# Scores and maxima in pairs, value and denominator batches in halves

## The chip, the core and the metric

The kernel runs on one core of one Trainium2 chip. The metric is the device time of one execution in microseconds, from launch to end. Five engines work side by side on that core: TensorE (matrix products), VectorE, ScalarE, GpSimd and SyncE, which issues most of the DMAs. Each runs its own list of instructions in order, and they wait for each other through semaphores.

## The reference, cut to what matters

A one-layer language model over 2 sequences of 2048 tokens, width 1024:

```python
h = b + sum(Wt[k][ctx[..., k]] for k in range(4))            # four table rows a token
h = h + attn(layernorm(h))                                   # 32 heads of 32, 8 key/value heads
h = h + ffn(layernorm(h))                                    # one product with a merged weight

# attention, for each of 2 x 32 heads; four heads share one key/value head
scores = q @ k.T / sqrt(32)                                  # 2048 x 2048, after rotary embedding
scores = where(causal, scores, -1e20)
out = softmax(scores, axis=-1) @ v
```

All of it is float32. The matrix products of attention's scores use a split of each operand in a high and a low part, stacked along the contracted rows: 96 rows are 3 x 32.

## The kernel before, in words

Three parts run one after the other: `part_a` (tables, layer norm, projections, rotary), `part_b` (attention) and `part_c` (output projection and last layer). The change is in `part_b` alone.

`part_b` works through 16 groups (`GROUPS`), a group being four query heads (`GROUP`) and the key/value head they share. The first and the last group are written out, the 14 between them are one loop (`groups`, L517). Queries are cut in four chunks of 512 (`QC`, `CT`), keys in tiles of 128. A **step** (`STEPS`, `score_steps`) is one chunk c of queries against one key tile kt, for the four heads: 40 steps a group. Each chunk begins with its four diagonal steps, in which only 512, 384, 256 and 128 queries see the key tile; then come its 4c full steps of 512. In a diagonal step a second small matmul with a mask is added to each score (L798).

The softmax subtracts the row maximum ahead of the exponential, so the maxima are computed first, one group's worth some 20 steps ahead (`LEAD`). For them queries are the rows: `MAXES` lists units (chunk, key chunk, query tile, head), 160 a group. TensorE computes one unit into one of four banks of PSUM (`row_scores`, L756), VectorE reduces it over its up to 512 keys into one column of `mpart` (`row_max`, L708). Behind the last unit of a chunk VectorE reduces `mpart` to `mcol`; TensorE transposes that (`turn`, L772), `TURN_AFTER` = 5 units later; VectorE splits the row in high and low part, and SyncE sends both into rows 96 and 97 of the queries `qs`, so that the score matmul of 98 rows subtracts the maximum by itself. `max_entries` writes units and turns in one list, spread over the steps; `entries_in` says which belong to a step.

In a step TensorE issues (`group`, L847):

- for each head h a score matmul into bank h mod 2 (`scores`, L785), which waits until ScalarE has taken the score two before it; behind it a quarter of the step's maxima entries (as a rule one), each of which waits until VectorE has done the entry four before it;
- after head 1 the value product of the step before the last (`values`, L801, `VALUE_LAG` = 2). Its output is 32 columns of the array wide for each head, and the four heads stand side by side in the array: four matmuls in float32, issued together, which the trace shows as eight records. I call this a value batch;
- at the end of every second step the denominators of a pair of steps (`denominators`, L814, `DEN_LAG` = 4): the same form, with ones in place of values, on the sum of two steps' probabilities that GpSimd made (L656). In a diagonal pair a batch over the 128 columns that only one step has stands ahead of it (L823).

```python
if not (is_first(g) and u < SCORE_BANKS):
    pe.wait_ge(exp_done, unit + u - (SCORE_BANKS - 1))
...
for h in range(GROUP):
    scores(g, unit, s, h)
    for more, n in entries[len(entries) * h // GROUP:len(entries) * (h + 1) // GROUP]:
        give(g + more, ring + more * NE, n)
    if h == GROUP // 2 - 1:
        lagging_values(g, unit, s)
lagging_denominators(g, pair, s)
```

ScalarE takes the exponentials one by one (`exps`, L667). At a chunk's end it also copies the value sums out of PSUM (`take_o`, L675) and the denominators (`take_den`, L680); the latter stands behind the first exponential of the step `DEN_LAG` + 1 behind the chunk's last (L691). The opening batch of the next chunk waits for these copies.

Of the kernel before, what the change touches and what calls it, by code (L numbers as in the profile page):

```python
# [17 lines left out]
P = 128  # L18
# [19 lines left out]
CT = 512  # L38
# [378 lines left out]
def max_units():  # L417

    return [(c, kc, t, h) for c in range(QC) for kc in range(c + 1) for t in range(TPC) for h in range(GROUP)]


STEPS, MAXES = score_steps(), max_units()
# [6 lines left out]
SCORE_BANKS, MAX_BANKS = 2, 4  # L429
VALUE_LAG, DEN_LAG = 2, 4  # L430
LEAD, FIRST_LEAD = 20, 14
TURN_AFTER = 5
# [30 lines left out]
def part_b(nc, q_hi, q_lo, k_hi, k_lo, v_dram, o_dram, den_dram, ident_in, mask_qk, mask_kq):  # L463

    with ExitStack() as ctx:
# [12 lines left out]
        mpart = sb("mpart", [P, GROUP * TPC, QC], F32)  # L478
        mcol = sb("mcol", [P, GROUP * TPC], F32)
# [7 lines left out]
        mx_ps = ctx.enter_context(nc.psum_tensor("mx_ps", [P, MAX_BANKS, CT], F32))  # L487
# [214 lines left out]
        def _(dve):  # L702
# [5 lines left out]
            def row_max(g, ring, n, unit):  # L708
# [3 lines left out]
                if unit - 1 in LAST_MAX or (unit == 0 and not is_first(g)):  # L712
                    dve.wait_ge(max_all, g * QC + c)
                nc.vector.tensor_reduce(mpart[:, h * TPC + t, kc:kc + 1], mx_ps[:, n % MAX_BANKS, 0:w], AX, ALU.max  # L714
                                        ).then_inc(max_done, 1)
                if unit in LAST_MAX:
                    dve.wait_ge(max_done, ring + n + 1)
                    nc.vector.tensor_reduce(mcol[:], mpart[:, :, 0:c + 1], AX, ALU.max).then_inc(max_all, 1)

            def maxima_rows(g, ring, n, c):  # L720

                mt_ps = mx_ps[0:GROUP * TPC, n % MAX_BANKS, 0:P]
# [8 lines left out]
            def take(g, ring, n):  # L731
                _, what, which = ENTRIES[n]
                if what == "max":
                    row_max(g, ring, n, which)
                else:
                    maxima_rows(g, ring, n, which)
# [13 lines left out]
        def _(pe):  # L750
            ring_count, unit_count = pe.alloc_register("pe_ring_count"), pe.alloc_register("pe_unit_count")
            step_count, pair_count = pe.alloc_register("pe_step_count"), pe.alloc_register("pe_pair_count")
# [3 lines left out]
            def row_scores(g, ring, n, unit):  # L756

                c, kc, t, h = MAXES[unit]
# [6 lines left out]
                out = mx_ps[:, n % MAX_BANKS, 0:w]  # L765
                mm = nc.tensor.matmul(out, qs[c][0:K_ROWS, h, t * P:(t + 1) * P],  # L766
                                      k_max[0:K_ROWS, kc * CT:kc * CT + w], start=True, stop=not diagonal)
                if diagonal:
                    mm = nc.tensor.matmul(out[:, w - P:w], identr, mqk, start=False, stop=True)  # L769
                mm.then_inc(max_ready, 1)  # L770

            def turn(g, n, c):  # L772
                pe.wait_ge(max_all, g * QC + c + 1)
                nc.tensor.transpose(mx_ps[0:GROUP * TPC, n % MAX_BANKS, 0:P], mcol[:], ident[:]).then_inc(max_ready, 1)

            def give(g, ring, n):
                _, what, which = ENTRIES[n]
                if not (is_first(g) and n < MAX_BANKS):
                    pe.wait_ge(max_done, ring + n - (MAX_BANKS - 1))
                if what == "max":  # L780
                    row_scores(g, ring, n, which)
# [504 lines left out]
```

## Time and profile before

| | us |
|---|---|
| median of 3 runs | 4025.11 |
| lowest, highest | 4018.99, 4042.11 |
| the profiled execution | 4027.74 |
| its span, first to last instruction | 4025.9 |

| engine | busy us | share of the span |
|---|---|---|
| TensorE, matmuls | 3776.8 | 94% |
| TensorE, weight loads | 2433.5 | 60% |
| VectorE | 2292.9 | 57% |
| ScalarE | 1626.7 | 40% |
| GpSimd | 1589.7 | 39% |

The profile is of one execution. Its page gives busy time by engine, then the span in 40 slices; other views group instructions by line and shape, sum them over a stretch, or list them in order of time. Matmul records overlap, since the array takes the next one while the last drains: a busy share near 100% isn't the array at its peak, and the pace is read from starts. Attention runs from about 740 us to 3200 us of the span.

### The profile page before, as it was taken

How to read it: one execution, taken by the hardware profiler on the slowest of the kernel's cores; microseconds unless marked ns; L12 is line 12 of the kernel's file. 1: busy time of each engine (PE TensorE's matmuls, PEld its weight loads, DVE VectorE, ACT ScalarE, POOL GpSimd, SP SyncE). 2: the span in 40 equal slices, each digit the busy share in tenths (PEclk: the TensorE clock that was granted, in tenths of full speed). 3: DMA queues.
4: the chain of work that ended last, by engine and by line, in shares of the span. 5: the costliest groups of instructions: out<-in, count | busy, mean ns of one | idle time of the engine just before them, and what ended most of it. 6: DMA issues, size and time to landing. Idle time of an engine off the chain costs nothing. (4 is left out here: it accounts for less than half of the span.)

```text
span 4025.9 us, 69672 instructions
## 1 busy us (share of the span) xinstructions
PE 3776.8 (94%) x22272; PEld 2433.5 (60%) x22272; DVE 2292.9 (57%) x3912; ACT 1626.7 (40%) x3068; POOL 1589.7 (39%) x525
## 2 busy tenths in 40 slices
PE   2889888899999999999999999999999779999999
PEld 2777777655555555555555555555555248888887
DVE  3666656676566566566566566566566144443443
ACT  2222222155555555555555555555555521010110
POOL 5222330045544544544544544545544513232322
PEclk9999999799999999999999999999999979999999
DMA  8877785411111111111111111111110243334432
GB/s 242 209 182 193 202 200 133 97 44 47 33 46 47 33 46 47 33 46 47 33 46 47 33 46 47 33 46 47 33 46 25 70 138 94 93 87 94 90 96 65
DMA packets 240124, 325.95 MB, mean 81 GB/s; under 512 B 62795, under 2 KB 139595, under 8 KB 239859
## 3 DMA queue, kind: packets, MB, share of 16 engines
q1 hardware_dynamic: 221426, 255.22, 23.7%
q0 software_dynamic: 18432, 67.12, 7.6%
q8 instruction: 177, 2.90, 0.3%
q14 instruction: 89, 0.72, 0.1%
HBM read 223.67 MB, written 97.52 MB: 80 GB/s over the span
## 5 line engine op out<-in xcount | busy, mean ns | idle before, releaser
L714 DVE TENSOR_REDUCE mpart<-mx_ps 128x1 f32<-128x512 f32 (+3 forms) x2560 | 1455.1, 606 | 841.4 <-PE mx_ps L769 455.3
L672 ACT ACTIVATE probs<-st_ps 128x512 f32<-128x512 f32 (+3 forms) x2560 | 1297.7, 533 | 1093.6 <-PE st_ps L798 535.7
L656 POOL TENSOR_TENSOR sums<-probs 128x2048 f32<-128x2048 f32 (+1 forms) x320 | 1182.6, 3696 | 1256.8 <-PE den_ps L827 1171.3
L795 PE MATMUL st_ps<-qs,k_score 98*128 98x512 f32 (+3 forms) x2560 | 1087.2, 428 | 31.2 <-issue 25.3
L766 PE MATMUL mx_ps<-k_max,qs 96*128 96x512 f32 (+3 forms) x2560 | 985.4, 393 | 14.5 <-POOL consts_r L647 14.1
L795 PEld LDWEIGHTS st_ps<-qs,k_score 98*128 98x128 f32 x2560 | 482.1, 189 | 814.5 <-ACT probs L672 659.6
L810 PE MATMUL o_ps<-probs,vs 128*32 128x512 f32 (+3 forms) x5120 | 606.9, 546 | 0.0
L766 PEld LDWEIGHTS mx_ps<-k_max,qs 96*128 96x128 f32 x2560 | 495.1, 195 | 48.2 <-POOL consts_r L647 14.3
L202 POOL DMA_INDIRECT hbuf<-in_tok_table,idx x128 | 194.1, 1517 | 352.3 <-ACT xn L233 231.2
L1030 POOL TENSOR_TENSOR h<-h,bb 128x1024 f32<-128x1024 f32 x32 | 105.1, 3283 | 543.2 <-DVE xn_c L1128 543.2
L386 PE MATMUL qk_ps<-x_hi,w_hi 128*128 128x512 f32 x640 | 259.7, 406 | 51.2 <-ACT rotation L245 31.8
L827 PE MATMUL den_ps<-sums,ones 128*32 128x512 f32 (+2 forms) x2560 | 284.1, 516 | 2.2 <-POOL sums L656 2.2
L386 PE MATMUL qk_ps<-x_lo,w_hi 128*128 128x512 f32 x640 | 256.6, 401 | 0.0
L386 PE MATMUL qk_ps<-x_hi,w_lo 128*128 128x512 f32 x640 | 255.9, 400 | 0.0
L798 PE MATMUL st_ps<-consts_r 128*128 128x128 f32 x1024 | 246.1, 240 | 5.9 <-issue 5.9
L769 PE MATMUL mx_ps<-consts_r 128*128 128x128 f32 x1024 | 246.0, 241 | 0.0
L769 PEld LDWEIGHTS mx_ps<-consts_r 128*128 128x128 f32 x1024 | 201.8, 197 | 28.4
L798 PEld LDWEIGHTS st_ps<-consts_r 128*128 128x128 f32 x1024 | 198.5, 194 | 22.6 <-issue 8.2
L1116 DVE TENSOR_TENSOR h<-oc_ps,h_in 128x1024 f32<-128x1024 f32 x32 | 39.2, 1225 | 289.6 <-PE oc_ps L1177 289.6
L810 PEld LDWEIGHTS o_ps<-probs,vs 128*32 128x32 f32 x5120 | 101.5, 108 | 151.7 <-ACT probs L672 84.2
L1054 ACT ACTIVATE std_c<-var_c 128x1 f32<-128x1 f32 x32 | 6.5, 203 | 434.2 <-DVE var_c L1123 434.2
L386 PEld LDWEIGHTS qk_ps<-x_hi,w_hi 128*128 128x128 f32 x640 | 125.1, 195 | 82.1 <-ACT rotation L245 34.7
(103 smaller groups left out, 3819.9 us busy)
## 6 DMA issues: line engine op xcount, KB each, us to landing
qs<-q_hi_scratch SPq DMA_DIRECT2D x128, 256.0 KB, 4.5
h_scratch<-hbuf SPq DMA_DIRECT2D x32, 512.0 KB, 3.5
q_hi_scratch<-rot_hi SPq DMA_DIRECT2D x64, 256.0 KB, 2.6
q_lo_scratch<-rot_lo SPq DMA_DIRECT2D x64, 256.0 KB, 3.3
qs<-q_lo_scratch SPq DMA_DIRECT2D x64, 256.0 KB, 5.5
o_scratch<-o_sb SPq DMA_DIRECT2D x64, 256.0 KB
o_in<-o_scratch SPq DMA_DIRECT2D x32, 512.0 KB, 4.4
o_in<-recip_scratch SPq DMA_DIRECT2D x128, 128.0 KB, 7.9
```

Of the source, the lines that this page charges most:

```text
L202: nc.gpsimd.indirect_dma_start(hbuf[:, t, :], None, tables[k], bass.IndirectOffsetOnAxis(ap=idx[:, j:j + 1], axis=0), compute_op=ALU.bypas ...
L386: mm = nc.tensor.matmul(qk_ps[:, f % 2, :], w[a], x[b], start=(c == 0 and k == 0), stop=(c == DC - 1 and k == 2))
L656: nc.gpsimd.tensor_tensor(sums[:, p % SUM_SLOTS, :, j * P:CT], a, b, ALU.add).then_inc(sum_done, 1)
L672: nc.scalar.activation(probs[:, s % SLOTS, h, j * P:CT], st_ps[:, u % SCORE_BANKS, 0:CT - j * P], ACT.Exp, scale=float(HD) ** -0.5).then_i ...
L714: nc.vector.tensor_reduce(mpart[:, h * TPC + t, kc:kc + 1], mx_ps[:, n % MAX_BANKS, 0:w], AX, ALU.max).then_inc(max_done, 1)
L766: mm = nc.tensor.matmul(out, qs[c][0:K_ROWS, h, t * P:(t + 1) * P], k_max[0:K_ROWS, kc * CT:kc * CT + w], start=True, stop=not diagonal)
L769: mm = nc.tensor.matmul(out[:, w - P:w], identr, mqk, start=False, stop=True)
L795: mm = nc.tensor.matmul(st_ps[:, u % SCORE_BANKS, 0:w], k_score[0:M_ROW + 2, kt * P:(kt + 1) * P], qs[c][0:M_ROW + 2, h, j * P:CT], start= ...
L798: mm = nc.tensor.matmul(st_ps[:, u % SCORE_BANKS, 0:P], identr, mkq, start=False, stop=True)
L810: mm = nc.tensor.matmul(o_ps[h * HD:(h + 1) * HD, j * P:CT], vs[:, kt, :], probs[:, s % SLOTS, h, j * P:CT], start=s in FIRST_OF, stop=s i ...
L827: mm = nc.tensor.matmul(den_ps[h * HD:(h + 1) * HD, at:CT], ones[:], sums[:, p % SUM_SLOTS, h, at:CT], start=False, stop=closing)
L1030: nc.gpsimd.tensor_tensor(h1[:, s, :], h1[:, s, :], bb[:], ALU.add).then_inc(h1b_done, 1)
```

## The change

Maxima are listed by pairs of heads (`max_pairs`, 80 a group). A pair has a slot of two banks, of which there are two; TensorE issues its two matmuls behind one wait, and VectorE reduces both with one instruction that writes two columns of `mpart`. A turn comes 3 pairs behind its chunk. Scores are issued in pairs too: heads 0 and 1, then 2 and 3, into the two banks, each pair behind one wait for all exponentials issued so far. Each half of a step is a score pair, half of the step's maxima entries, and a part of the value batch, now of the step before (`VALUE_LAG` = 1): columns up to 384 (`VALUE_SPLIT`) in the first half, the rest in the second; the wait for its exponentials is gone, since the score pair ahead has waited for them. Behind the second half comes half of a denominator batch, every step. The diff, without the renamings on VectorE and with its other declarations cut:

```diff
+def max_pairs():
...
+    return [(c, kc, t, h) for c in range(QC) for kc in range(c + 1) for t in range(TPC) for h in range(0, GROUP, 2)]
...
-SCORE_BANKS, MAX_BANKS = 2, 4
-VALUE_LAG, DEN_LAG = 2, 4
+SCORE_BANKS, MAX_SLOTS = 2, 2
+VALUE_LAG, DEN_LAG = 1, 4
+VALUE_SPLIT = 3 * P
 LEAD, FIRST_LEAD = 20, 14
-TURN_AFTER = 5
+TURN_AFTER = 3
...
-        mpart = sb("mpart", [P, GROUP * TPC, QC], F32)
+        mpart = sb("mpart", [P, GROUP, TPC, QC], F32)
...
-        mx_ps = ctx.enter_context(nc.psum_tensor("mx_ps", [P, MAX_BANKS, CT], F32))
+        mx_ps = ctx.enter_context(nc.psum_tensor("mx_ps", [P, MAX_SLOTS, 2, CT], F32))
...
-                nc.vector.tensor_reduce(mpart[:, h * TPC + t, kc:kc + 1], mx_ps[:, n % MAX_BANKS, 0:w], AX, ALU.max
+                nc.vector.tensor_reduce(mpart[:, h:h + 2, t, kc], mx_ps[:, n % MAX_SLOTS, :, 0:w], AX, ALU.max
                                         ).then_inc(max_done, 1)
-                if unit in LAST_MAX:
...
-            def row_scores(g, ring, n, unit):
-
-                c, kc, t, h = MAXES[unit]
-                if t == 0 and h == 0 and kc == 0:
+            def pair_scores(g, n, pair):
+
+                c, kc, t, first_head = MAXES[pair]
+                if t == 0 and first_head == 0 and kc == 0:
                     pe.wait_ge(q_loaded[c], LOAD * (g + 1))
-                if t == 0 and h == 0 and kc == c:
+                if t == 0 and first_head == 0 and kc == c:
                     pe.wait_ge(k_max_loaded[c], LOAD * (g + 1))
                 diagonal = kc == c
                 w = (t + 1) * P if diagonal else CT
-                out = mx_ps[:, n % MAX_BANKS, 0:w]
-                mm = nc.tensor.matmul(out, qs[c][0:K_ROWS, h, t * P:(t + 1) * P],
-                                      k_max[0:K_ROWS, kc * CT:kc * CT + w], start=True, stop=not diagonal)
-                if diagonal:
-                    mm = nc.tensor.matmul(out[:, w - P:w], identr, mqk, start=False, stop=True)
+                for k in range(2):
+                    out = mx_ps[:, n % MAX_SLOTS, k, 0:w]
+                    mm = nc.tensor.matmul(out, qs[c][0:K_ROWS, first_head + k, t * P:(t + 1) * P],
+                                          k_max[0:K_ROWS, kc * CT:kc * CT + w], start=True, stop=not diagonal)
+                    if diagonal:
+                        mm = nc.tensor.matmul(out[:, w - P:w], identr, mqk, start=False, stop=True)
                 mm.then_inc(max_ready, 1)
 
...
-                if not (is_first(g) and n < MAX_BANKS):
-                    pe.wait_ge(max_done, ring + n - (MAX_BANKS - 1))
+                if not (is_first(g) and n < MAX_SLOTS):
+                    pe.wait_ge(max_done, ring + n - (MAX_SLOTS - 1))
...
-            def scores(g, unit, s, h):
+            def scores(g, unit, s, first_head):
 
                 c, kt, j = STEPS[s]
-                u, w = s * GROUP + h, CT - j * P
+                w = CT - j * P
                 diagonal = kt >= c * TPC
-                if s in FIRST_OF and h == 0:
+                if s in FIRST_OF and first_head == 0:
                     pe.wait_ge(m_rows, 32 * (g * QC + c + 1))
                     pe.wait_ge(k_score_loaded[c], LOAD * (g + 1))
-                if not (is_first(g) and u < SCORE_BANKS):
-                    pe.wait_ge(exp_done, unit + u - (SCORE_BANKS - 1))
-                mm = nc.tensor.matmul(st_ps[:, u % SCORE_BANKS, 0:w], k_score[0:M_ROW + 2, kt * P:(kt + 1) * P],
-                                      qs[c][0:M_ROW + 2, h, j * P:CT], start=True, stop=not diagonal)
-                if diagonal:
-                    mm = nc.tensor.matmul(st_ps[:, u % SCORE_BANKS, 0:P], identr, mkq, start=False, stop=True)
-                mm.then_inc(st_ready, 1)
-
-            def values(g, unit, s):
+                if not (is_first(g) and s == 0 and first_head == 0):
+                    pe.wait_ge(exp_done, unit + s * GROUP + first_head)
+                for h in range(first_head, first_head + 2):
+                    bank = h % SCORE_BANKS
+                    mm = nc.tensor.matmul(st_ps[:, bank, 0:w], k_score[0:M_ROW + 2, kt * P:(kt + 1) * P],
+                                          qs[c][0:M_ROW + 2, h, j * P:CT], start=True, stop=not diagonal)
+                    if diagonal:
+                        mm = nc.tensor.matmul(st_ps[:, bank, 0:P], identr, mkq, start=False, stop=True)
+                    mm.then_inc(st_ready, 1)
+
+            def values(g, s, part):
 
                 c, kt, j = STEPS[s]
-                pe.wait_ge(exp_done, unit + GROUP * (s + 1))
-                if s in FIRST_OF:
+                if s in FIRST_OF and part == 0:
                     pe.wait_ge(v_loaded[c], 16 * (g + 1))
                     if not (is_first(g) and c == 0):
                         pe.wait_ge(o_copied, g * QC + c)
-                for h in range(GROUP):
-                    mm = nc.tensor.matmul(o_ps[h * HD:(h + 1) * HD, j * P:CT], vs[:, kt, :],
-                                          probs[:, s % SLOTS, h, j * P:CT], start=s in FIRST_OF, stop=s in LAST_OF)
-                mm.then_inc(pv_done, 1)
-
-            def denominators(g, pair, p):
+                lo, hi = ((j * P, VALUE_SPLIT), (max(j * P, VALUE_SPLIT), CT))[part]
+                if lo < hi:
+                    for h in range(GROUP):
+                        mm = nc.tensor.matmul(o_ps[h * HD:(h + 1) * HD, lo:hi], vs[:, kt, :],
+                                              probs[:, s % SLOTS, h, lo:hi], start=s in FIRST_OF and part == 0,
+                                              stop=s in LAST_OF and part == 1)
+                if part == 1:
+                    mm.then_inc(pv_done, 1)
+
+            def denominators(g, pair, p, part):
 
                 c, kt, j = STEPS[2 * p]
                 diagonal, opening, closing = kt >= c * TPC, 2 * p in FIRST_OF, 2 * p + 1 in LAST_OF
-                pe.wait_ge(sum_done, pair + p + 1)
-                if opening and not (is_first(g) and c == 0):
-                    pe.wait_ge(den_copied, g * QC + c)
-                if diagonal:
+                alone = (j * P, (j + 1) * P) if diagonal else (0, 0)
+                half = (j * P + CT) // 2 if diagonal else CT // 2
+                if part == 0:
+                    pe.wait_ge(sum_done, pair + p + 1)
+                    if opening and not (is_first(g) and c == 0):
+                        pe.wait_ge(den_copied, g * QC + c)
+                    if diagonal:
+                        for h in range(GROUP):
+                            nc.tensor.matmul(den_ps[h * HD:(h + 1) * HD, alone[0]:alone[1]], ones[:],
+                                             probs[:, 2 * p % SLOTS, h, alone[0]:alone[1]], start=opening, stop=False)
+                lo, hi = ((alone[1], half), (half, CT))[part]
+                if lo < hi:
                     for h in range(GROUP):
-                        nc.tensor.matmul(den_ps[h * HD:(h + 1) * HD, j * P:(j + 1) * P], ones[:],
-                                         probs[:, 2 * p % SLOTS, h, j * P:(j + 1) * P], start=opening, stop=False)
-                at = (j + 1) * P if diagonal else 0
-                for h in range(GROUP):
-                    mm = nc.tensor.matmul(den_ps[h * HD:(h + 1) * HD, at:CT], ones[:],
-                                          sums[:, p % SUM_SLOTS, h, at:CT], start=False, stop=closing)
-                mm.then_inc(den_done, 1)
-
...
-                    for h in range(GROUP):
-                        scores(g, unit, s, h)
-                        for more, n in entries[len(entries) * h // GROUP:len(entries) * (h + 1) // GROUP]:
+                    for part in range(2):
+                        scores(g, unit, s, 2 * part)
+                        for more, n in entries[len(entries) * part // 2:len(entries) * (part + 1) // 2]:
                             give(g + more, ring + more * NE, n)
-                        if h == GROUP // 2 - 1:
-                            lagging_values(g, unit, s)
+                        lagging_values(g, s, part)
                     lagging_denominators(g, pair, s)
```

## Rows read from the trace of the kernel before

**Rows 1.** The page, part 2: granted clock of TensorE in tenths, 40 slices.

```profile
PEclk9999999799999999999999999999999979999999
```

**Rows 2.** Busy time by stretch: each engine's us and count, granted clock, DMA.

```profile
1000.00:3000.00 2000.00, 1967.71 (x13187) 1068.19 (x13187) 1237.17 (x2274) 1119.68 (x2223) 979.38 (x265) 0.99 0.16 42
```

**Rows 3.** Groups by shape, 1000 to 3000 us: busy, mean ns; idle before, releasers.

```profile
L714 DVE TENSOR_REDUCE mpart<-mx_ps 128x1 f32<-128x512 f32 x1468 | 934.9, 685 | 394.4 <-PE mx_ps L766 319.3 <-PE mx_ps L769 73.6
L672 ACT ACTIVATE probs<-st_ps 128x512 f32<-128x512 f32 x1492 | 836.2, 596 | 595.9 <-PE st_ps L795 438.1 <-PE st_ps L798 144.9
L656 POOL TENSOR_TENSOR sums<-probs 128x2048 f32<-128x2048 f32 x160 | 732.0, 4575 | 567.4 <-PE den_ps L827 531.8 <-ACT probs L672 35.5
...
L682 ACT COPY den_sb<-den_ps 128x512 f32<-128x512 f32 x53 | 30.8, 580 | 0.0
```

**Rows 4.** The same stretch, TensorE, shapes of a line together.

```profile
L795 PE MATMUL st_ps<-qs,k_score 98*128 98x512 f32 (+3 forms) x2119 | 904.6, 428 | 26.4 <-issue 25.3
```

**Rows 5.** Timeline of TensorE: start, duration, line, instruction; full steps without and with denominators.

```profile
2133.76 1.06 PE L810 MATMUL o_ps<-probs,vs 128*32 128x512 f32 x8
2134.75 0.50 PE L795 MATMUL st_ps<-qs,k_score 98*128 98x512 f32 x1
2135.09 0.40 PE L766 MATMUL mx_ps<-k_max,qs 96*128 96x512 f32 x1
2135.32 0.40 PE L795 MATMUL st_ps<-qs,k_score 98*128 98x512 f32 x1
2135.56 0.39 PE L766 MATMUL mx_ps<-k_max,qs 96*128 96x512 f32 x1
2135.94 0.50 PE L795 MATMUL st_ps<-qs,k_score 98*128 98x512 f32 x1
2136.28 0.40 PE L766 MATMUL mx_ps<-k_max,qs 96*128 96x512 f32 x1
...
2136.76 0.39 PE L766 MATMUL mx_ps<-k_max,qs 96*128 96x512 f32 x1
2137.08 1.07 PE L810 MATMUL o_ps<-probs,vs 128*32 128x512 f32 x8
...
2141.35 0.64 PE L810 MATMUL o_ps<-probs,vs 128*32 128x512 f32 x4
```

**Rows 6.** Timeline of TensorE: narrow batches, in the last group.

```profile
3157.23 0.43 PE L810 MATMUL o_ps<-probs,vs 128*32 128x128 f32 x8
3157.59 0.91 PE L795 MATMUL st_ps<-qs,k_score 98*128 98x512 f32 x2
3158.42 0.43 PE L823 MATMUL den_ps<-probs,ones 128*32 128x128 f32 x8
3158.66 0.83 PE L827 MATMUL den_ps<-sums,ones 128*32 128x384 f32 x8
3159.42 0.73 PE L795 MATMUL st_ps<-qs,k_score 98*128 98x512 f32 x2
```

**Rows 7.** Timeline of ScalarE beside rows 5.

```profile
2133.25 1.08 ACT L672 ACTIVATE probs<-st_ps 128x512 f32<-128x512 f32 x2 [1.11 <-PE st_ps L795]
2135.29 2.27 ACT L672 ACTIVATE probs<-st_ps 128x512 f32<-128x512 f32 x4 [0.96 <-PE st_ps L795]
```

**Rows 8.** Timeline of VectorE beside rows 5.

```profile
2135.52 2.48 DVE L714 TENSOR_REDUCE mpart<-mx_ps 128x1 f32<-128x512 f32 x4 [0.83 <-PE mx_ps L766]
```

**Rows 9.** Chain of waits that ended last: one last-layer product of 48 matmuls.

```profile
3314.57 10.88 PE f_ps L1177 x48
```

**Rows 10.** Timeline of TensorE: first score matmul of a loop pass.

```profile
1998.90 0.55 PE L795 MATMUL st_ps<-qs,k_score 98*128 98x512 f32 x1 [2.05 <-issue]
```

**Rows 11.** Timeline of TensorE: value batches of the last group, without maxima.

```profile
3172.72 1.07 PE L810 MATMUL o_ps<-probs,vs 128*32 128x512 f32 x8
...
3175.82 1.07 PE L810 MATMUL o_ps<-probs,vs 128*32 128x512 f32 x8
...
3179.14 1.07 PE L810 MATMUL o_ps<-probs,vs 128*32 128x512 f32 x8
```

More of the change, by code:

```diff
@@ L414, in score_steps @@
             for kt in list(range(c * TPC, (c + 1) * TPC)) + list(range(c * TPC))]
-def max_units():
-    return [(c, kc, t, h) for c in range(QC) for kc in range(c + 1) for t in range(TPC) for h in range(GROUP)]
-STEPS, MAXES = score_steps(), max_units()
+def max_pairs():
+    return [(c, kc, t, h) for c in range(QC) for kc in range(c + 1) for t in range(TPC) for h in range(0, GROUP, 2)]
+STEPS, MAXES = score_steps(), max_pairs()
 NS, NM = len(STEPS), len(MAXES)
@@ L477, in part_b @@
         den_sb = sb("den_sb", [P, 2, CT], F32)
-        mpart = sb("mpart", [P, GROUP * TPC, QC], F32)
-        mcol = sb("mcol", [P, GROUP * TPC], F32)
+        mpart = sb("mpart", [P, GROUP, TPC, QC], F32)
+        mcol = sb("mcol", [P, GROUP, TPC], F32)
         m_hi = sb("m_hi", [GROUP * TPC, P], F32R)
@@ L706, in _, with pair_max @@
             nc.vector.memset(ones[:], 1.0).then_inc(ones_done, 1)
-            def row_max(g, ring, n, unit):
-                c, kc, t, h = MAXES[unit]
+            def pair_max(g, ring, n, pair):
+                c, kc, t, h = MAXES[pair]
                 w = CT if kc < c else (t + 1) * P
                 dve.wait_ge(max_ready, ring + n + 1)
-                if unit - 1 in LAST_MAX or (unit == 0 and not is_first(g)):
+                if pair - 1 in LAST_MAX or (pair == 0 and not is_first(g)):
                     dve.wait_ge(max_all, g * QC + c)
-                nc.vector.tensor_reduce(mpart[:, h * TPC + t, kc:kc + 1], mx_ps[:, n % MAX_BANKS, 0:w], AX, ALU.max
+                nc.vector.tensor_reduce(mpart[:, h:h + 2, t, kc], mx_ps[:, n % MAX_SLOTS, :, 0:w], AX, ALU.max
                                         ).then_inc(max_done, 1)
-                if unit in LAST_MAX:
+                if pair in LAST_MAX:
                     dve.wait_ge(max_done, ring + n + 1)
-                    nc.vector.tensor_reduce(mcol[:], mpart[:, :, 0:c + 1], AX, ALU.max).then_inc(max_all, 1)
+                    nc.vector.tensor_reduce(mcol[:], mpart[:, :, :, 0:c + 1], AX, ALU.max).then_inc(max_all, 1)
             def maxima_rows(g, ring, n, c):
-                mt_ps = mx_ps[0:GROUP * TPC, n % MAX_BANKS, 0:P]
+                mt_ps = mx_ps[0:GROUP * TPC, n % MAX_SLOTS, 0, 0:P]
                 dve.wait_ge(max_ready, ring + n + 1)
@@ L733, in take @@
                 if what == "max":
-                    row_max(g, ring, n, which)
+                    pair_max(g, ring, n, which)
                 else:
@@ L780, in give @@
                 if what == "max":
-                    row_scores(g, ring, n, which)
+                    pair_scores(g, n, which)
                 else:
                     turn(g, n, which)
-            def scores(g, unit, s, h):
+            def scores(g, unit, s, first_head):
                 c, kt, j = STEPS[s]
-                u, w = s * GROUP + h, CT - j * P
+                w = CT - j * P
                 diagonal = kt >= c * TPC
-                if s in FIRST_OF and h == 0:
+                if s in FIRST_OF and first_head == 0:
@@ new lines, in denominators, with lagging_values @@
+                lo, hi = ((alone[1], half), (half, CT))[part]
+                if lo < hi:
+                    for h in range(GROUP):
+                        mm = nc.tensor.matmul(den_ps[h * HD:(h + 1) * HD, lo:hi], ones[:],
+                                              sums[:, p % SUM_SLOTS, h, lo:hi], start=False,
+                                              stop=closing and part == 1)
+                if part == 1:
+                    mm.then_inc(den_done, 1)
+            def lagging_values(g, s, part):
@@ L832, in lagging_values @@
                 k = s - VALUE_LAG
                 if k >= 0:
-                    values(g, unit, k)
+                    values(g, k, part)
                 elif not is_first(g):
-                    values(g - 1, unit - NU, k + NS)
+                    values(g - 1, k + NS, part)
             def lagging_denominators(g, pair, s):
                 k = s - DEN_LAG
-                if k % 2 == 0:
-                    return
                 if k >= 0:
-                    denominators(g, pair, k // 2)
+                    denominators(g, pair, k // 2, k % 2)
@@ L844, in lagging_denominators @@
                 elif not is_first(g):
-                    denominators(g - 1, pair - PAIRS, (k + NS) // 2)
+                    denominators(g - 1, pair - PAIRS, (k + NS) // 2, k % 2)
             def group(g, first, last):
@@ L864, in _ @@
             last = GROUPS - 1
-            for s in range(NS, NS + DEN_LAG + 1):
-                if s - VALUE_LAG < NS:
-                    lagging_values(last, last * NU, s)
-                if s - DEN_LAG < NS:
-                    lagging_denominators(last, last * PAIRS, s)
+            pe.wait_ge(exp_done, GROUPS * NU)
+            for s in range(NS, NS + DEN_LAG):
+                for part in range(2):
+                    if s - VALUE_LAG < NS:
+                        lagging_values(last, s, part)
+                lagging_denominators(last, last * PAIRS, s)
 def part_c(nc, o_dram, den_dram, recip_dram, h_dram, w_o_t, b_o, w_base_t, b_base, enc, coefs, mask,
```

7 lines of the change are left out of this document (3 added, 4 removed).

## The prediction, made before the kernel ran

> **What bounds the kernel now.** I read the page first, then the busy time by stretches, the groups of instructions of the attention stage, and the timelines of single engines. The page's slices show a granted clock of nine tenths or more in all but two, so TensorE is at 2.4 GHz [rows 1]. In 1000 to 3000 us, wholly inside attention, TensorE is busy 1967.7 of 2000 us, VectorE 1237, ScalarE 1120, GpSimd 979 [rows 2]. The idle time of VectorE and ScalarE ends on TensorE [rows 3]: attention runs at TensorE's pace. "Busy" hides something, though: starts show the pace, durations overlap. 2119 score matmuls at 160 a group are 13.24 groups, so a group (40 steps) takes 151.0 us [rows 4].
>
> Where it goes is read from starts [rows 5]. A 512-wide score or maxima matmul follows the last one by 0.235 us (2135.09 to 2135.32 and on). The value batch costs more than its columns: it starts 0.32 after the matmul before it (2136.76 to 2137.08), the next score starts 1.00 after it (2133.76 to 2134.75), and the matmul behind that score comes 0.34 later (2134.75 to 2135.09). The widths give what is columns: a batch of 128 takes 0.36 to the next score (3157.23 to 3157.59) [rows 6], one of 512 takes 1.00, so 128 columns are 0.213 and 0.145 is fixed. With 0.085 on the way in and 0.105 behind, entering and leaving the 32-column form costs **0.33 us a visit**. Two batches in one visit cost nothing extra: 128 then 384 wide take 0.24 + 0.76 = 1.00 (3158.42 to 3159.42), as one of 512 does [rows 6].
>
> The waits for ScalarE are small. Value batches start at 2133.76, 2137.08 and 2141.35: 3.32 us for a step without denominators, 4.27 with them [rows 5]. A denominator visit is 0.33 + 0.853 = 1.18, so without a stall both would be 3.09: the first stalls 0.23. It stands between the last maxima matmul and the next score (2135.56 to 2135.94, 0.38 for 0.235), and in the cold weight load behind (0.34 for 0.235).
>
> **The change, per group of 40 steps.**
>
> *Matmul work.* The same score, maxima and mask matmuls and columns. Value and denominator columns are the same too, in more and narrower batches: no column cost.
>
> *Visits.* Before: 40 value and 20 denominator batches, each between score or maxima matmuls, 60 visits. After: value part 0 (up to column 384) in the first half of each step, except behind the four steps whose width is 128, where it is empty: 36; value part 1 and half a denominator batch side by side in the second half: 40. That is 16 more x 0.33 = **+5.3 us**. The bounds of one visit are 0.145 (only the fixed part is real, the rest slack) and 0.33: +2.3 to +5.3; I take 0.33, since at 2134.75 to 2135.09 nothing is waited for and the 0.105 is still there.
>
> The Trainium skill, "TensorEngine Tiling (Array Packing)", Key Properties, says that changing the tiling mode drains TensorE. The trace agrees: 0.33 a visit, nothing between two batches in the same mode [rows 5, 6]. By the rule the change pays 16 more drains, the +5.3; had the 0.085 in front of a value batch been its semaphore wait, which part 0 drops, 36 x 0.085 = 3.1 would come off.
>
> *Full steps.* Half one: score, score, maxima, maxima take 0.34 + 0.235 + 0.235 + 0.32 = 1.13, then a batch of 384 columns takes 0.145 + 0.64 = 0.78: 1.91. Half two: the same 1.13, then 128 + 256 columns in one visit, 0.78 again: 1.91. A step is 3.82, two are 7.65; before two take 3.32 + 4.27 = 7.59.
>
> *Score waits.* A pair waits until both exponentials of the pair before are done. From the first score's start to its exponential is 0.54 (2134.75 to 2135.29), two exponentials take 1.08 [rows 7], and from an exponential's end to the released score is 0.05 (2135.29 + 0.60 to 2135.94) [rows 3, 5, 7]: the chain is 1.67, under 1.91, hidden in full halves. So the old stall goes: 0.23 x 20 steps without denominators is at most 4.6, less in diagonal steps; I take **-4.0** (bounds 0 and -6).
>
> *Where the cover is gone.* In the four steps behind a 128-wide step, half one has no value batch: 0.34 + 3 x 0.235 = 1.05. In these very steps (DEN_LAG + 1 behind a chunk's end) ScalarE copies the denominators between exponential 0 and 1 (L691), 0.58 [rows 3]. The chain is 0.54 + 0.60 + 0.58 + 0.60 + 0.05 = 2.37; the second pair is 1.32 late, and its weights load cold (0.105): 4 x 1.43 = **+5.7**. Before, scores 2 and 3 wait for one exponential each, with a value batch in between. Bounds: 0.62 x 4 = 2.5 (the copy costs nothing) and 5.7; the copy stands in ScalarE's order, so the upper. Half one of the step whose only entry is the turn has no maxima: 0.34 + 0.32 + 0.78 = 1.44 against 1.67, **+0.2**. The opening value batch waits for ScalarE's copy: with lag 1 the copy comes in the half ahead of part 0, and ends before it.
>
> *Maxima.* A reduction of 512 takes 0.69 alone, 2.48 for four back to back [rows 3, 8]. One over 1024 isn't shown: bounds 1.07 (elements at 0.133 per 128, no start cost) and 1.38 (two alone); I take 1.24, the back-to-back row. Two slots of pairs give TensorE a step from giving pair n to wanting its slot: 0.70 + 1.24 of 3.82. Nothing, either way. VectorE paces the 14 steps of maxima ahead of the loop; about 28 pairs save up to 0.1 each: -2 once.
>
> *Waits dropped.* 80 score, 80 maxima and 40 value waits fewer. A matmul in the last layer, which waits for nothing, goes at 10.88 / 48 = 0.227 [rows 9]; here it is 0.235 with the wait met. Bounds 0 and 0.008 x 200 = 1.6 off; I take 0, since this stream's own spacing is the nearer row and half of the waits stay in it.
>
> *GpSimd* adds 4.6 us every two steps (7.6) [rows 3]; part 0 of a denominator wants its sum one step earlier, still a step after it is made. *SP* sends the same DMAs in the same order; the turn comes 6 score units behind a chunk instead of 5, with steps to spare. *Loop end.* TensorE has 2.05 us of "issue" at each new group [rows 10]; it stays.
>
> **Sum.** +5.3 - 4.0 + 5.7 + 0.2 = +7.2 a group, x 15.5 (the last group has maxima for half its steps) = +112. Its last 20 steps, without maxima, run 3.10 + 3.32 = 6.42 per two now [rows 11] and 4 x 1.67 = 6.68 after: +3. Less 2 ahead of the loop: +113. The profiled span 4025.9 becomes 4139; 1.8 lie around it, so 4140.7 against 4027.7, and that execution stood 2.6 above the median of the runs: 4138.
>
> **Rivals.**
> A, *faster*: the dispatch of a waiting instruction is the hidden price, all over attention. 200 fewer waits a group decide from 7.2 / 200 = 36 ns each; at 50 ns, -10 + 7.2 = -2.8, x 15.5: 3982. For it: 0.235 against 0.227, and 0.38 where a wait really holds. Against: 8 ns is a fifth of what is wanted, and scores whose wait is met start on time [rows 5, 9].
> B, *no change*: the copy costs nothing (+2.5 in place of +5.7), and the removed stalls are 6: 5.3 - 6 + 2.5 + 0.2 = +2, less 1.6 for waits: +0.4, 4031. For it: two full steps differ by 0.06. Against: it needs three ends at once.
> C, *much slower*: the reduction over two heads is slow and two slots bind. From 1.91 a pair VectorE is the bound; at 2.2, +0.29 x 80 = 23 a group, 4490. Nothing in the rows suggests it but that the form is new.
>
> **How the numbers follow.** Forecast 78% (own range 4070 to 4195: per-group +2.8 to +11, the upper end by taking removed stalls at 1 and as much again in diagonal halves), A 9%, B 10%, C 3%. Half a per cent, 20 us, is about what a measurement of this kernel tells from no change. Slower by more: forecast and C, 0.80; same: B and a little of the forecast's low end, 0.11; faster: 0.09. The range 4045 to 4195 leaves A, most of B and C out.
>
> **What would show it.** Step right: matmul starts 0.33 apart around each visit, four per two steps; a group at 158 us (2000 us hold 12.65 of them); TensorE at 3.82 a full step in both halves; the stall of 1.3 behind the 128-wide steps, with the denominators' copy in it. Wrong: a group under 151 us, a score following a score in under 0.227, pair reductions above 1.4, or a visit cheaper than 0.33 where its wait is gone.

## The result and the profile after

| | before | after |
|---|---|---|
| median us | 4028.97 | 4326.95 |
| lowest, highest | 4018.99, 4042.11 | 4303.75, 4376.22 |
| the profiled execution, its span | 4027.74, 4025.9 | 4342.14, 4340.3 |

The ratio is 1.0723 (95% interval 1.0662 to 1.0784): slower by 7.2%, where 2.7% was forecast. The side was right and 4327 us lies outside the range of 4045 to 4195. The highest run of the changed kernel, 4376.22 us at a granted clock of 0.918, counts as a slow one and is left out of the ratio.

The granted clock by slices (page, part 2) and the busy time of 1000 to 3000 us, to be laid beside [rows 1, 2]:

```profile
PEclk9999999599999998899889989989979978999999
```

```profile
1000.00:3000.00 2000.00, 1880.77 (x16608) 1113.89 (x16606) 1035.48 (x1082) 964.55 (x1977) 870.01 (x236) 0.93 0.14 37
```

TensorE is busy for less of the stretch though it is handed more instructions, and the mean granted clock fell from 0.99 to 0.93. With two levels, 2.4 and 1.2 GHz, 0.93 is half clock for 14% of the time, 280 us of these 2000. The groups of the same stretch, where the change has them [rows 3, 4]:

```profile
L715 DVE TENSOR_REDUCE mpart<-mx_ps 128x2 f32<-128x1024 f32 x659 | 805.7, 1226 | 486.5 <-PE mx_ps L768 380.2 <-PE mx_ps L771 104.9
L800 PEld LDWEIGHTS st_ps<-qs,k_score 98*128 98x128 f32 x1883 | 328.2, 198 | 569.7 <-ACT probs L673 360.2 <-issue 203.9
```

A reduction over two heads takes 1.23 us, as taken in the sum (1.24). 1883 scores in 2000 us are 169.9 us a group, 18.9 more than before; 7.2 were forecast. Full steps at full clock are not to blame. TensorE's timeline in full steps:

```profile
2121.45 0.72 PE L800 MATMUL st_ps<-qs,k_score 98*128 98x512 f32 x2
2122.02 0.62 PE L768 MATMUL mx_ps<-k_max,qs 96*128 96x512 f32 x2
2122.57 0.85 PE L816 MATMUL o_ps<-probs,vs 128*32 128x384 f32 x8
2123.35 0.73 PE L800 MATMUL st_ps<-qs,k_score 98*128 98x512 f32 x2
2123.92 0.63 PE L768 MATMUL mx_ps<-k_max,qs 96*128 96x512 f32 x2
2124.48 0.43 PE L816 MATMUL o_ps<-probs,vs 128*32 128x128 f32 x8
2124.72 0.61 PE L839 MATMUL den_ps<-sums,ones 128*32 128x256 f32 x8
2125.27 0.72 PE L800 MATMUL st_ps<-qs,k_score 98*128 98x512 f32 x2
```

The halves take 1.90 and 1.92 us, the step 3.82, to the hundredth what was worked out. The group's end is another matter. TensorE and SyncE there, beside [rows 10]:

```profile
2140.35 0.61 PE L839 MATMUL den_ps<-sums,ones 128*32 128x256 f32 x8
...
2147.34 0.77 PE L800 MATMUL st_ps<-qs,k_score 98*128 98x512 f32 x1 [6.38 <-issue]
```

```profile
2139.57 0.80 SPq L533 DMA_DIRECT2D qs<-q_hi_scratch  x2
2140.51 0.40 SPq L533 DMA_DIRECT2D qs<-q_lo_scratch  x1
```

TensorE waits 6.38 us for nothing that the profile names ("issue"), where it was 2.05. The stretches behind it, ten microseconds each (the last columns: granted clock, DMA share, GB/s):

```profile
2130.00:2140.00 10.00, 10.00 (x84) 5.24 (x82) 6.36 (x6) 5.91 (x12) 4.62 (x2) 1.00 0.03 9
2140.00:2150.00 10.00, 3.62 (x30) 2.63 (x33) 0.88 (x3) 1.38 (x3) 4.49 (x1) 0.64 0.43 103
2150.00:2160.00 10.00, 10.00 (x53) 6.32 (x46) 2.09 (x3) 3.28 (x7) 0.00 (x0) 0.50 0.03 8
...
2180.00:2190.00 10.00, 10.00 (x65) 5.52 (x64) 4.24 (x5) 2.89 (x6) 0.36 (x1) 0.50 0.08 29
...
2210.00:2220.00 10.00, 10.00 (x92) 5.20 (x95) 6.28 (x6) 6.22 (x12) 6.00 (x2) 1.00 0.09 22
```

Behind the stall the clock is at its lower level and stays there until 2208, with TensorE busy all the time. This is one of the two longest: behind the first score of the 13 loop passes that follow a branch back, the half clock lasts 4 to 61 us, 25 on average. In the kernel before it is 0 to 7, 2 on average. What it costs is seen by laying two passes side by side, from first score to first score:

```profile
1466.70:1628.80 162.10, 151.66 (x1412) 89.65 (x1413) 88.04 (x92) 81.46 (x168) 73.86 (x20) 0.98 0.15 39
2147.30:2333.30 186.00, 176.54 (x1412) 104.41 (x1412) 88.12 (x92) 82.70 (x168) 73.82 (x20) 0.83 0.14 34
```

The same matmuls take 162.1 us at a granted clock of 0.98 and 186.0 at 0.83.

### The profile page after: what moved, and what is told of

The parts are those of the page before. It is cut to its first block and busy times, and to the rows that moved or that the text cites. A ratio compares the mean times of both kernels' runs of the same rounds, so it can differ in the third digit from the quotient of the medians.

```text
span 4340.3 us, 78343 instructions
## 1 busy us (share of the span) xinstructions
PE 3966.6 (91%) x28928; PEld 2660.7 (61%) x28928; DVE 2202.4 (51%) x2632; ACT 1586.6 (37%) x3068; POOL 1590.1 (37%) x525
## 5 line engine op out<-in xcount | busy, mean ns | idle before, releaser
L715 DVE TENSOR_REDUCE mpart<-mx_ps 128x2 f32<-128x1024 f32 (+3 forms) x1280 | 1360.0, 1066 | 1228.7 <-PE mx_ps L771 709.0
L673 ACT ACTIVATE probs<-st_ps 128x512 f32<-128x512 f32 (+3 forms) x2560 | 1250.3, 532 | 1423.4 <-PE st_ps L803 748.3
L800 PE MATMUL st_ps<-qs,k_score 98*128 98x512 f32 (+3 forms) x2560 | 969.9, 445 | 152.9 <-issue 82.7
L800 PEld LDWEIGHTS st_ps<-qs,k_score 98*128 98x128 f32 x2560 | 450.4, 200 | 769.1 <-ACT probs L673 492.9
L768 PE MATMUL mx_ps<-k_max,qs 96*128 96x512 f32 (+3 forms) x2560 | 869.6, 410 | 18.6 <-POOL consts_r L648 14.3
L816 PE MATMUL o_ps<-probs,vs 128*32 128x128 f32 (+2 forms) x9728 | 760.7, 387 | 0.2 <-ACT probs L673 0.2
L816 PEld LDWEIGHTS o_ps<-probs,vs 128*32 128x32 f32 x9728 | 196.1, 110 | 352.1 <-issue 321.4
L839 PE MATMUL den_ps<-sums,ones 128*32 128x256 f32 (+1 forms) x4608 | 346.1, 374 | 2.7 <-POOL sums L657 2.7
L803 PEld LDWEIGHTS st_ps<-consts_r 128*128 128x128 f32 x1024 | 225.8, 221 | 0.1
L1189 PE MATMUL oc_ps<-wc_hi,a_hi 128*128 128x512 f32 x512 | 162.8, 399 | 9.9 <-DVE a_lo L1117 9.9
```

Source lines behind the costliest of these rows:

```text
L673: nc.scalar.activation(probs[:, s % SLOTS, h, j * P:CT], st_ps[:, u % SCORE_BANKS, 0:CT - j * P], ACT.Exp, scale=float(HD) ** -0.5).then_i ...
L715: nc.vector.tensor_reduce(mpart[:, h:h + 2, t, kc], mx_ps[:, n % MAX_SLOTS, :, 0:w], AX, ALU.max).then_inc(max_done, 1)
L768: mm = nc.tensor.matmul(out, qs[c][0:K_ROWS, first_head + k, t * P:(t + 1) * P], k_max[0:K_ROWS, kc * CT:kc * CT + w], start=True, stop=no ...
L800: mm = nc.tensor.matmul(st_ps[:, bank, 0:w], k_score[0:M_ROW + 2, kt * P:(kt + 1) * P], qs[c][0:M_ROW + 2, h, j * P:CT], start=True, stop= ...
L803: mm = nc.tensor.matmul(st_ps[:, bank, 0:P], identr, mkq, start=False, stop=True)
L816: mm = nc.tensor.matmul(o_ps[h * HD:(h + 1) * HD, lo:hi], vs[:, kt, :], probs[:, s % SLOTS, h, lo:hi], start=s in FIRST_OF and part == 0, ...
```

## The experiments

Twelve kernels, timed beside the kernel before, whose medians in their three sessions were 4035.78, 4036.97 and 4035.76. (The changed kernel was timed beside the 4028.97 above.) Three readings of each stand in one table: the mean granted clock of 960 to 3100 us, the us a group in that stretch (2140 x 160 over the score matmuls in it), and the "issue" waits of score matmuls there (how many, and their sum).

| kernel | median us | ratio | clock | us a group | issue waits |
|---|---|---|---|---|---|
| before | 4035.8 | 1 | 0.99 | 150.7 | 13, 25.3 |
| after | 4326.95 | 1.072 | 0.93 | 169.5 | 12, 76.1 |
| e1 after, load late | 4345.45 | 1.078 | 0.91 | 169.9 | 12, 41.3 |
| e2 before, load late | 4036.47 | 1.001 | 0.98 | 151.4 | 13, 25.9 |
| e3 before, split batches | 4232.5 | 1.051 | 0.93 | 164.9 | 12, 59.9 |
| e4 after, whole batches | 4256.0 | 1.054 | 0.96 | 165.3 | 12, 27.1 |
| e5 after, no loop | 4130.13 | 1.023 | 1.00 | 155.4 | none |
| e6 before, no loop | 3984.87 | 0.987 | 1.00 | 147.3 | none |
| e7 before, long stall | 4120.54 | 1.021 | 0.97 | 156.3 | DMA, 79.4 |
| e8 after, copy later | 4317.01 | 1.073 | 0.91 | 170.5 | 12, 75.0 |
| e9 after, last step whole | 4316.44 (one run) | | 0.92 | 169.2 | 24, 50.2 |
| e10 after, code shifted | 4337.88 (one run) | | 0.93 | 169.4 | 12, 68.8 |
| e11 before, no loop, joined | 3942.23 | 0.977 | 1.00 | 144.6 | none |
| e12 before, no loop, split | 4059.65 | 1.006 | 1.00 | 151.9 | none |

**e1 and e2, the load moved behind the loop end.**

```diff
-                    after_scores(V_LAST[2])
+                    sp.wait_ge(st_ready, unit + NU + 1)
+                    pass_waits(sp, sp_passed)
                     load_q(g + 1, 3)
```

> The changed kernel with one edit: SyncE issues the load of the last query chunk (and of the third key chunk behind it) only when the first score of the next group is done, instead of when the last scores of this group are done. Theory A (TensorE's code for the next loop pass comes by DMA and stands behind this load): the stall of 5.7 to 7.0 us at each loop end falls to 1.5 to 3 us, the stretches at half clock behind it become shorter, and the time is 4100 to 4260 us. Rival B (the fetch itself is long, because the loop's code is longer): the stall stays at 6 to 7 us and the time within 0.5% of the changed kernel's. Rival C (the extra time sits in the steps): the stall may fall, but the time by under 70 us.

> The kernel before with the same edit of the load. Theory A: its stall of 2.05 us at the loop end is already ahead of the load, so it stays at 1.5 to 2.1 us; time 3995 to 4035 us. Rival B the same. If the load late in the group were itself a cost (maxima of the last chunk waiting for it), over 4040 us.

The stall of the changed kernel nearly halved, to 3.4 us a loop end, and the time did not move (ratio 1.0779, 1.0720 to 1.0839). Theory A had the side of the stall right but not its size (1.5 to 3 us), and the time wrong; rival B had the time right and the stall wrong; rival C fits both readings here and is taken up with e5. e2 is the kernel before in time (1.0006, 0.9989 to 1.0022) and in its stalls of 2.0 us. One loop end of e1 and the stretches behind it:

```profile
2152.65 0.77 PE L801 MATMUL st_ps<-qs,k_score 98*128 98x512 f32 x1 [3.42 <-issue]
```

```profile
2150.00:2160.00 10.00, 7.35 (x40) 4.83 (x40) 1.39 (x2) 2.81 (x5) 3.85 (x1) 0.61 0.43 102
2160.00:2170.00 10.00, 10.00 (x52) 6.91 (x48) 1.92 (x2) 2.82 (x7) 2.13 (x1) 0.50 0.02 7
2170.00:2180.00 10.00, 10.00 (x65) 6.19 (x68) 4.38 (x5) 1.87 (x6) 1.31 (x1) 0.50 0.02 5
2180.00:2190.00 10.00, 9.70 (x85) 5.48 (x77) 5.57 (x7) 4.99 (x10) 1.28 (x1) 0.85 0.43 104
```

The load ahead of TensorE's code is about 3 us of the 6.4, and 3.4 are left without it, against about 2 in e2. But the clock comes down behind 3.4 us as it does behind 6.4: 7 to 61 us at half clock behind a loop end, 32 on average.

**e3 and e4, one half of the change each.** e3 gives the kernel before the two functions of the change for value and denominator batches, e4 gives the changed kernel back those of before.

```diff
-                        if h == GROUP // 2 - 1:
-                            lagging_values(g, unit, s)
+                        if h % 2:
+                            lagging_values(g, unit, s, h // 2)
```

> The kernel before with the value and denominator batches split as in the change, and nothing else (single scores and maxima, value lag 2). Price of a visit 0.33 us: 76 visits a group instead of 60 give +5.3, the stalls of up to 4 us a group at the scores go: +1 to +5 a group, 4040 to 4110 us, full steps of 3.82 us. If splitting alone brings the long stall at the loop end (Rival B, longer code; the matmul count is that of the change): a stall of 6 us and 4150 us or more; by theory A the stall is 2 to 4 us.

> The changed kernel with whole value and denominator batches again (values in the first half of each step, denominators behind every second step), pairs of scores and maxima kept: code as short as before. By the chain of 1.67 us from a score pair to the next, a full step without denominators takes 2.13 + 1.67 = 3.80 and one with them 4.26, so 8.06 for two, +9 a group against before: 4170 us plus what the loop end adds. Rival B (code length makes the stall): stall 2 us. Theory A (order of load and fetch): the stall stays above 4 us, if TensorE gets to its loop end 1.4 us or more after the load's issue.

Split batches alone bring the long stall (5.0 us each) and 1.0505 (1.0454 to 1.0556). Pairs alone, the 1.67 us chain uncovered in the second half of each step, cost 1.0542 (1.0510 to 1.0575) with a stall of 2.3 us; two full steps take 8.05 us, where 8.06 was worked out. Theory A had asked for more than 4 us in e4, since the load is issued 1.6 us ahead of the last batch's end there too; rival B, longer code, fits e3 and e4 better. What both left out is when TensorE's code comes. The trace has it as packets of 16 KB on one queue (q8 of the page), which I take for TensorE's, since writing out TensorE's loop alone changes their number (177 to 135 for the kernel before, 226 to 187 for the changed one). The last such packet ahead of the first score starts, over the 13 loop ends of each kernel and counted from the last batch's end: before 0.7 to 1.3 us ahead of it, e4 0.5 to 1.0 ahead; e1 0.2 to 0.5 behind it; e3 1.3 to 2.4 and after 2.4 to 4.2 behind it, the load's packets being under way. From that packet's end to the first matmul of the pass it is always the same: 1.7 to 2.3 us, 2.0 on average, at all 117 loop ends of the nine kernels that keep the loop and have no added wait (e7). So the stall is the packet's arrival plus 2 us, whether it is 1.6 or 7.3 us long.

**e5, e6, e12: no loop.** TensorE's groups are written out in a row; the other engines keep their loops. e12 is e3 in this form.

```diff
-            groups(pe, group)
+            for g in range(GROUPS):
+                group(g, g == 0, g == GROUPS - 1)
```

> The changed kernel with TensorE's 16 groups written out in a row instead of a loop (same instructions, no branch; the other engines keep their loops). Theory A (the loop end's stall of 6 us, and the half clock that follows it, carry what the prediction missed): no stalls of 1.2 us or more at the group ends, half clock in attention under 50 us, 4110 us (4080 to 4150): the 4027 of before, plus 95 to 112 for the steps, less 25. Rival B (the half clock comes from the shape of the steps, pairs and split batches, and only shows first behind a stall): half clock stays over 200 us and the time over 4200 us.

> The kernel before with TensorE's groups written out. Its 13 stalls of 2 us and the clock behind them go: 25 + 18 us less, 3985 us (3975 to 4010). If code fetched in a straight line stalls TensorE elsewhere, 4025 us or more.

> The kernel before with split batches (as e3), groups written out. By e3, whose steps outside loop ends and half clock cost 2.35 us a group more than before: e6 + 38 = 4023 us (4010 to 4040), and what is left to e5's 4130 us belongs to issuing in pairs. If the split itself brings the half clock: over 4060 us.

e5 and e6 came within 20 and 1 us of what was expected: 1.0233 (1.0212 to 1.0254) and 0.9865 (0.9843 to 0.9887). The same steps as in the changed kernel, without a break at the group's end, run at full clock from 851 us on, but for two dips of 3 and 7 us. Rival B is out, and so is rival C of e1 for what the loop end adds. The page's clock line of e5:

```profile
PEclk9999999689999999999999999999999969999999
```

One part of theory A missed: half clock in attention under 50 us. Attention starts at half clock in all these kernels, behind a pause (in e5 TensorE is busy for 1.6 of the 10 us from 740), and the one with the changed steps keeps it longer, until 851 us of the span where e6 is back at 809. e5, then e6:

```profile
740.00:850.00 110.00, 91.39 (x397) 61.97 (x399) 57.06 (x64) 18.52 (x39) 9.93 (x5) 0.52 0.28 59
```

```profile
740.00:850.00 110.00, 94.71 (x486) 63.93 (x484) 77.98 (x143) 30.64 (x62) 20.79 (x8) 0.72 0.36 76
```

So the first group takes 182.5 us in e5 and 157.0 in e6. Two other profiles with the changed steps, e8 and e10, are back at 801 and 814, and their first group takes 161.9 and 163.0: the 20 us are the clock's and not the steps'.

e12 took 37 us more than expected (1.0061, 1.0039 to 1.0082). The split costs 4060 - 3985 = 75 us, and pairs the other 4130 - 4060 = 70. Of the 75, 59 are in the 14 groups behind the first, at full clock, 4.2 a group; 20 are in the first group, which is at half clock until 844. Of the 70, 50 are in the 14 groups, 3.6 each.

**e7, a long stall in the steps of before.**

```diff
+                if s == 0 and h == 0 and not is_first(g):
+                    pe.wait_ge(q_loaded[QC - 1], LOAD * (g + 1))
```

> The kernel before with a wait added at each group's first score for the load of the last query chunk, issued at the end of the group before: a stall of 4 to 7 us in place of 2 at each group. Theory A (a long stall drops the clock for long, whatever the steps look like): 60 to 75 us of stalls more and 100 us or more lost to the clock, 4180 to 4230 us. Rival B (the shape of the steps): the stalls alone, 4090 to 4110 us.

A stall nearly as long as the changed kernel's (6.1 us, and also at the two group starts without a branch back) cost 84 us, 1.0205 (1.0181 to 1.0229): 10 us over rival B's range and 60 under theory A's. The stretches behind one stall, the one with the shortest half clock:

```profile
2360.00:2370.00 10.00, 5.26 (x25) 3.39 (x25) 1.14 (x3) 1.88 (x4) 3.60 (x1) 0.66 0.34 86
2370.00:2380.00 10.00, 10.00 (x74) 6.00 (x72) 6.06 (x12) 5.01 (x12) 3.47 (x1) 1.00 0.03 8
```

Here the clock is back 4 us behind the first score; over the 15 stalls of e7 it takes 4 to 17 us, 8 on average, where the changed kernel has 4 to 61 and 25. A break brings the clock down in either kernel; in the steps of before it comes back soon, in the changed ones often late. The first group shows the same without a loop end.

**e8, the copy of the denominators one exponential later.**

```diff
-                        if h == 0 and k % NS in LAST_OF and not (first and k < 0):
+                        if h == 1 and k % NS in LAST_OF and not (first and k < 0):
```

> The changed kernel with ScalarE's copy of the denominators behind exponential 1 instead of exponential 0. By the prediction's term the chain in the four steps behind a 128-wide step falls from 2.37 to 1.67 us: the longest waits of a full-clock group (a score 1.28 to 1.39 us behind the maxima) fall to 0.7, about 0.6 to 0.7 x 4 = 2.6 a group, 40 us off, with the loop ends and clock as they fall. Rival: the copy was not in the way: no change.

The wait was where the prediction put it. The changed kernel, from the score pair of such a step to the next, then e8, the end of the same:

```profile
2094.16 0.73 PE L800 MATMUL st_ps<-qs,k_score 98*128 98x512 f32 x2
...
2095.27 0.58 ACT L683 COPY den_sb<-den_ps 128x512 f32<-128x512 f32 x1
...
2096.40 0.72 PE L800 MATMUL st_ps<-qs,k_score 98*128 98x512 f32 x2 [1.11 <-ACT probs L673]
```

```profile
2247.97 1.08 ACT L673 ACTIVATE probs<-st_ps 128x512 f32<-128x512 f32 x2 [1.47 <-PE st_ps L800]
...
2249.11 0.73 PE L800 MATMUL st_ps<-qs,k_score 98*128 98x512 f32 x2 [0.62 <-ACT probs L673]
```

The chain is 2.24 us where 2.37 was worked out; in e8 it is 1.75 (2247.36 to 2249.11), and the wait falls by 0.49, four times a group. In the time that is 2 us a group against the clock's scatter: 1.0733 (1.0668 to 1.0797) is no difference from the changed kernel.

**e9 and e10, what the loop end is like.**

```diff
-                        lagging_values(g, s, part)
+                        if s < NS - 1:
+                            lagging_values(g, s, part)
+                        elif part == 0:
+                            lagging_values(g, s, 0)
+                            lagging_values(g, s, 1)
```

> The changed kernel, loop kept, with the value batch of the group's last step whole in the first half, so that a group ends in a half denominator batch alone (16 matmul records and weight loads fewer at the end). Theory A1 (TensorE's sequencer can run only so many instructions ahead, and narrow batches at the end keep it from the branch): the packet of TensorE's code at the loop end starts before the last batch ends, as in the kernel before, and the stall falls from 6 to 2 to 3 us. Theory A2 (where the branch lies in the 16 KB blocks of code): the stall moves somewhere else or stays at 6 us, without a pattern.

```diff
+            for k in range(64):
+                nc.tensor.matmul(o_ps[:, 0:P], identr, mqk, start=True, stop=True)
```

> The changed kernel with 64 small matmuls more ahead of the first maxima, which only shift the loop's code by about 128 instructions, half a 16 KB block. Theory A2: the stall at the loop end changes by more than 1 us. Theory A1: it stays at 6 to 7 us.

In e9 the packet of code starts 0.4 to 0.7 us ahead of the last batch's end and the stall is 2.4 to 3.0 us, theory A1's pattern, though a second one of 0.9 to 2.2 us appears some 5 us on:

```profile
2167.71 0.47 PE L800 MATMUL st_ps<-qs,k_score 98*128 98x512 f32 x1 [2.98 <-issue]
...
2172.05 0.79 PE L800 MATMUL st_ps<-qs,k_score 98*128 98x512 f32 x1 [1.38 <-issue]
```

In e10 ten of 13 stalls are 5.5 to 7.1 us long, near the 6 to 7 of A1, and three are 3.8 to 4.6, so where the code lies may have a part too, but does not cure it. Neither theory of the sequencer is shown: e9 moves the packet by the last step's instructions, and no run says why. The time of both (one run each) is the changed kernel's, as the clock is: in e9 breaks of 2.7 us are followed by 3 to 61 us at half clock, 26 on average.

**e11, a version that beats both.**

```diff
                         if h == GROUP // 2 - 1:
                             lagging_values(g, unit, s)
-                    lagging_denominators(g, pair, s)
+                            lagging_denominators(g, pair, s)
```

> The kernel before, groups written out, with the denominator batch right behind the value batch in every second step instead of at its end: 40 visits a group instead of 60, the scores of every step now meeting the stall of 0.23 us at the exponentials. By the price of 0.33 us a visit: -6.6 + 4.6 = -2.0 a group, 32 us under e6: 3953 us (3935 to 3975). Rival (the price belongs to the batch, not to the visit): nothing saved, the stalls added, 4050 us or more.

The loop is written out as in e6. 3942 us, 0.9765 (0.9736 to 0.9795) of before, and 43 us under e6 where 32 were worked out from the price of a visit. One joined visit:

```profile
2061.70 0.22 PE L769 MATMUL mx_ps<-consts_r 128*128 128x128 f32 x1
2061.86 0.43 PE L810 MATMUL o_ps<-probs,vs 128*32 128x128 f32 x8
2062.10 0.40 PE L823 MATMUL den_ps<-probs,ones 128*32 128x128 f32 x8
2062.32 0.83 PE L827 MATMUL den_ps<-sums,ones 128*32 128x384 f32 x8
2063.07 0.50 PE L795 MATMUL st_ps<-qs,k_score 98*128 98x512 f32 x1
```

Three batches of 640 columns in all take 1.21 us to the next score: 1.07 of columns and the exit once.

## Why the prediction was wrong

Without the loop the two kernels are 4130.1 - 3984.9 = 145 us apart; as they stand, 4327 - 4037 = 290. The other 145 are what the loop end adds to the changed kernel over what it adds to the one before (197 against 52). Of them 13 x (6.3 - 1.9) = 57 us are the stalls themselves, and the 88 that are left go with the clock behind them: found by subtraction, and borne out by the two passes of 162 and 186 us above.

The 145 without the loop are not all steps. From first score to first score the 14 groups behind the first take 147.6 us each in e6 and 155.4 in e5: 7.8 a group, 109 in all. The first group is 25 us longer, about 18 of it the longer half clock at attention's start. The rest lies at the two ends. Of the 290, 113 were forecast; the 177 that were missed are 57 of stalls and 88 of clock at the loop ends, 18 of clock at attention's start and 14 in the steps and at the ends.

- **Loop end** ("TensorE has 2.05 us of issue at each new group; it stays") is the step that failed. It grew to 6.3 us, and the sum had no term for the clock at all, though [rows 1] were read: full clock was taken as given, at the loop end and at attention's start. The sum asked what the moved instructions wait for, but not when TensorE's own code comes: its packet starts 2.4 to 4.2 us behind the last batch's end with the group's load ahead of it, and 0.2 to 0.5 behind it without (e1). The Trainium skill, "Runtime: NRT & Kernel Launch", Instruction fetch mechanics, says that a taken branch to code that isn't at hand forces a DMA fetch before execution goes on; e5 and e6, in which the stalls vanish with the branch, agree.
- **Visits** held their price: the full steps (3.82) contain two, and e11 shows it from the other side. So did the **chain** (2.24 for 2.37) and **maxima** (1.23 for 1.24).
- **The sum of the steps**, 7.2 us a group, measured 7.8, and that is luck in part, since two terms were mis-sized and cancel. Split batches were sized at 5.3 - 4.0 = 1.3 us a group and cost 59 / 14 = 4.2 (e12 over e6): with visits at 0.33, only 1.1 of the 4.0 of old stalls went. Where the stall was read it goes whole: two full steps near the group's end take 7.57 in e6 and 7.68 in e12 (medians over twelve groups), where 7.59 was read and 7.65 worked out. But it was counted for all 20 pairs of steps, and most had less to lose: the last two diagonal steps of the third chunk go from 6.96 to 7.26. Pairs were sized at 5.7 + 0.2 = 5.9 and cost 50 / 14 = 3.6 (e5 over e12): the wait is there four times a group, but the two steps around it are 0.8 to 1.3 us longer than in e12, 4.1 for the four and not 5.7, and the other steps a little shorter.
- **Rival A** (waits cost) is out: e5 has all the dropped waits and is slower. **Rival C** is out by the 1.23. **Rival B** needed the stalls of before to be 6 us a group, and 1.1 went.

Why the clock comes back late in the changed steps is not settled. It is not the stall's length alone (e1 and e7 cross), nor the loop end (the first group of e5 and e12). Split batches alone do it (e3, 0.93; 21 us behind a loop end) and pairs alone less (e4, 0.96, with stalls of 2.3; 12 us). It also differs from one pass of the same kernel to the next. That TensorE's code comes later when the batches are split hangs on the last step's instructions, as e9 shows; why is open.

## What to carry to other kernels

Read the loop end as a step of its own: list what is issued in the last microsecond before the branch on every queue, and ask whether the engine's own code must come behind it. Price any stall at the engine's clock as well as at its length, by the granted clock of the stretches behind the stalls that are there already. Work in another shape of the array is paid by the visit, so gather it before spreading it.

## What the runs showed that was not expected

- Writing out TensorE's 16 groups is worth 52 us before the change and 197 after it, and no other stall of TensorE came in its place.
- A break of 3.4 us (e1) was followed by as much half clock as one of 6.4 (0.91 and 0.93 on average), while a break of 6 us in the steps of before (e7) left 0.97.
- In the first two groups, with no branch back ahead of them, the changed kernel is at half clock from 743 to 849 us of the span and then holds full clock to the first loop end at 1128. Four of six profiles with the changed steps show this (e8 and e10 do not), and the loop does not explain it.
- At 117 loop ends of nine kernels the first matmul came 1.7 to 2.3 us after the packet of code had landed, whatever the stall.
